# Edge passes of a graph-attention kernel: one accumulating transfer for two tiles, rings of six

## The reference

```python
def _gatv2(x, src, dst, Wl, bl, Wr, br, att, bias):
    xl = (x @ Wl + bl).reshape(N, H, C)
    xr = (x @ Wr + br).reshape(N, H, C)
    e = leaky_relu(xl[src] + xr[dst], 0.2)
    logits = einsum('ehc,hc->eh', e, att)
    m = segment_max(logits, dst)
    p = exp(logits - m[dst])
    s = segment_sum(p, dst)
    alpha = p / s[dst]
    return segment_sum(xl[src] * alpha[..., None], dst).reshape(N, H * C) + bias
```

## Time and profile before

| | us |
|---|---|
| median of 3 runs | 3033.68 |
| lowest and highest run | 3030.25, 3037.02 |
| profiled execution, its own time | 3031.11 |
| span of the profiled execution, first to last instruction | 3029.4 |
| busy: PE, DVE, ACT, POOL | 2627.9, 2517.6, 1696.8, 1318.7 |

### The profile page before, as it was taken

The page is one execution under the profiler, slowest core; times in us unless marked ns, Lnnn a source line. Parts: engine busy times, 40 slices in busy tenths (PEclk is TensorE's granted clock), DMA queues, the critical chain, the costliest instruction groups (busy, mean ns, idle before and its releaser), DMA issues. The chain is left out here.

```text
span 3029.4 us, 41062 instructions
## 1 busy us (share of the span) xinstructions
PE 2627.9 (87%) x11205; PEld 1800.7 (59%) x11205; DVE 2517.6 (83%) x5677; ACT 1696.8 (56%) x4291; POOL 1318.7 (44%) x1218
## 2 busy tenths in 40 slices
PE   6999999788888089999988888861899999969997
PEld 5777777333333078888864333320688888846665
DVE  7989998699999466677757999994988888469997
ACT  3545555277777433333323777774778877525554
POOL 0012220688887133333327888862333333014443
PEclk8999999899999599999999999985899999989998
DMA  8989999588887488888756888875999999469999
GB/s 321 341 305 320 319 324 339 185 233 240 236 240 209 116 274 276 268 269 264 263 200 205 235 240 239 241 188 169 386 357 354 348 345 346 148 176 252 249 252 158
DMA packets 332704, 789.73 MB, mean 261 GB/s; under 512 B 55118, under 2 KB 55664, under 8 KB 322266
## 3 DMA queue, kind: packets, MB, share of 16 engines
q1 hardware_dynamic: 220440, 540.20, 51.1%
q0 software_dynamic: 109584, 243.11, 33.4%
q10 hardware_dynamic: 2452, 3.79, 0.4%
HBM read 469.66 MB, written 329.28 MB: 264 GB/s over the span
## 5 line engine op out<-in xcount | busy, mean ns | idle before, releaser
L888 PE MATMUL bank<-wr,nT_e 128*128 128x512 f32 x1280 | 607.0, 619 | 0.5 <-DVE z_e L747 0.5
L1045 PE MATMUL bank<-whi,t_hi 128*128 128x512 f32 x1256 | 524.9, 418 | 23.9 <-DVE t_lo L406 23.9
L1047 PE MATMUL bank<-whi,t_lo 128*128 128x512 f32 x1256 | 499.3, 398 | 0.0
L1046 PE MATMUL bank<-wlo,t_hi 128*128 128x512 f32 x1256 | 498.9, 397 | 0.0
L888 PEld LDWEIGHTS bank<-wr,nT_e 128*128 128x128 f32 x1280 | 243.2, 200 | 250.5 <-issue 250.5
L912 POOL DMA_INDIRECT vin<-touched,node_slot x157 | 172.7, 1100 | 336.2 <-DMA vin<-rows 328.8
L912 POOL DMA_INDIRECT g_vin<-touched,node_slot x157 | 174.6, 1112 | 327.1 <-DMA g_xin<-in_x 303.7
L642 POOL DMA_INDIRECT nv_e<-rows,dst_row x160 | 209.9, 1312 | 175.5 <-POOLq L81 129.8
L1045 PEld LDWEIGHTS bank<-whi,t_hi 128*128 128x128 f32 x1256 | 237.9, 189 | 74.0 <-issue 17.4
L984 ACT CAST t_hi<-bank 128x512 fp32r<-128x512 f32 (+1 forms) x157 | 91.8, 585 | 329.7 <-PE bank L1047 329.6
L1047 PEld LDWEIGHTS bank<-whi,t_lo 128*128 128x128 f32 x1256 | 237.9, 189 | 58.8
(11 more groups left out here) (245 smaller groups left out, 6293.1 us busy)
## 6 DMA issues: line engine op xcount, KB each, us to landing
rows<-t_row SPq DMA_DIRECT2D x312, 512.0 KB, 4.4
w_e<-w_e POOLq DMA_DIRECT2D x160, 256.0 KB
touched<-done_e SPq DMA_DIRECT2D x160, 256.0 KB
xin<-in_x SPq DMA_DIRECT2D x156, 256.0 KB, 4.7
xTin<-in_xT SPq DMA_DIRECT2D x156, 256.0 KB
vin<-rows SPq DMA_DIRECT2D x156, 256.0 KB, 4.0
g_vin<-rows SPq DMA_DIRECT2D x156, 256.0 KB
g_xin<-in_x SPq DMA_DIRECT2D x156, 256.0 KB
```

The lines of the kernel that those rows point to most:

```text
L888: pe.matmul(psR[b][:, :], nT[:, b, cc, :], wr[:, cc, :], start=(cc == 0), stop=False)
L1045: pe.matmul(ps, hi[:, cc, :], whi[:, cc, :], start=(cc == 0), stop=False)
L1046: pe.matmul(ps, hi[:, cc, :], wlo[:, cc, :], start=False, stop=False)
L1047: last = pe.matmul(ps, lo[:, cc, :], whi[:, cc, :], start=False, stop=(cc == KC - 1))
```

## The change

The accumulating transfer is issued once for tiles 2u and 2u + 1, when the second of them is weighed (and for the last tile alone if their number is odd, which it isn't here). It covers two neighbouring slots of the rings, 4 KB in a partition. The rings have six slots, `w_added` has one semaphore for each pair of slots, and its starting value in layer 1 is counted for each pair. `accumulate` stands one turn later (lag G + 3 = 8).

```diff
-WR = 4
+WR = 6
...
-        g["w_added"] = [ctx.enter_context(nc.semaphore(f"w_added{u}")) for u in range(WR)]
+        g["w_added"] = [ctx.enter_context(nc.semaphore(f"w_added{u}")) for u in range(WR // 2)]
...
-        w_added, w0 = g["w_added"], layer * 16 * len(range(0, T, WR))
+        w_added, w0 = g["w_added"], [layer * 16 * len(range(2 * u, T, WR)) for u in range(WR // 2)]
...
             def add_own(t):
-                b = t % WR
+                if t % 2 == 0 and t < T - 1:
+                    return
+                b, n = t // 2 * 2 % WR, t % 2 + 1
                 pool.wait_ge(s["weighted"], t + 1)
-                pool.dma_start(w1[:, b, :], w2[:, b, :], accum_op=ALU.add).then_inc(w_added[b], 16)
+                pool.dma_start(w1[:, b:b + n, :], w2[:, b:b + n, :], accum_op=ALU.add).then_inc(w_added[b // 2], 16)
...
             def accumulate(t):
                 i, b = t // G, t % WR
-                dve.wait_ge(w_added[b], w0 + 16 * (t // WR + 1))
+                dve.wait_ge(w_added[b // 2], w0[b // 2] + 16 * (t // WR + 1))
...
-            lag = G + 2
+            lag = G + 3
```

## The result

The changed kernel takes 3017.46 us (median of five runs, 3016.2 to 3018.03), the kernel before 3033.01 beside it: a ratio of 0.9949, 95% interval 0.9936 to 0.9962. The profiled execution has a span of 3015.7 against 3029.4. The forecast was 3021, with 3000 to 3037 as its range. The time came out close, but not by the forecast's terms, as the rows show.

The account below looks back on a forecast made before the run. DVE was taken as the bound, with collisions behind POOL; -17.9 us from collisions and +5.8 at the ends make -12.1, from 3031.1 to 3019.0, and 2.6 for the median gives 3021 us, range 3000 to 3037.

Parts of the forecast that it names:

- What bounds, and the collision: DVE's loop: DVE is the bound; L757 stands behind POOL's L655, 1.12 us each, 32 times, 16 in a pass.
- The price of a double issue: L650 on POOL: issuing a transfer of two tiles costs 0.98 us, as a single one does; by tile 1.97.
- How many collisions go: DVE and POOL in the loops: 8 of 16 in a pass go, saving 17.9 us; bounds 12 to 20 in all.
- the start: Start of a pass: POOL still works off its lead of gathers, which may move the count by two or three either way.
- No wait for PE in the loop: DVE in the loop: it never waits for PE, whose 2.9 us to spare shrink to 0.9.
- PE starves: Rival, PE's gathers in the loop: DVE waits for PE once in ten tiles, 16 x 1 us: 3037; 0.17 with nothing gained.
- The later `accumulate` and the rings, at zero: DVE and ACT in the loop: moving `accumulate` a turn later and rings of six each change the time by zero.
- The ends of the passes: Serial end of each pass: costs 2.9 us a pass, 5.8 for both; bounds 2.4 to 10.
- the exponentials of the last group: ACT at the end of each pass: they come about 0.7 us later.
- the second `scale`: End of each pass: `scale(78)` must also wait for the last transfer, some +1.17 us.
- the transfer's growth: End of each pass: the last transfer carries two tiles, 256 KB more, +1.03 us.
- The sum: Whole kernel: -17.9 from collisions and +5.8 at the ends make -12.1 us.

Follow-up runs that it names:

- the long memset: The kernel before, with POOL's multiplication L655 replaced by a memset of a spare tile of 128 x 1344 elements: 3004.17 us, ratio 0.9905.
- the run on the ends: The changed kernel with a transfer of its own for each of the last two tiles of a pass: 3009.74 us, ratio 0.9923.

## Why the prediction was right

**What bounds, and the collision.** Right: an L655 with a lead, 1.12 us each. The long memset shows that a POOL which is merely busy and first does not do it.

**The price of a double issue.** Right: 0.96 us, where 0.98 was taken.

**How many collisions go.** The step that was mis-sized: 24 of 32 went, not 16, beyond the bounds of 12 to 20. Its reasoning holds in the steady part, where a collision is left once in ten tiles; with PE never late there are six a pass. What it missed lies at the start. The 16 of a pass are not one in each group of five: the first nine tiles have none, and four fall on tiles 9, 10, 13 and 14 (605.44 to 634.42 in pass 0). These eight of the 32 come where `accumulate` has hardly begun and a DVE turn can be as short as 4.07 us:

```profile
597.92 1.22 DVE L752 SCALAR_TENSOR_TENSOR z_e<-z_e 128x1024 f32<-128x1024 f32 x1
601.99 1.22 DVE L752 SCALAR_TENSOR_TENSOR z_e<-z_e 128x1024 f32<-128x1024 f32 x1
605.44 1.80 DVE L757 TENSOR_TENSOR z_e<-z_e,v_att 128x512 f32<-128x512 f32 x1
...
595.17 1.28 POOL L655 TENSOR_TENSOR z_e<-z_e,v_att 128x512 f32<-128x512 f32 x1 [0.96 <-DVE z_e L752]
600.20 1.31 POOL L655 TENSOR_TENSOR z_e<-z_e,v_att 128x512 f32<-128x512 f32 x1
605.39 1.30 POOL L655 TENSOR_TENSOR z_e<-z_e,v_att 128x512 f32<-128x512 f32 x1
```

A turn of POOL with a transfer is 5.03 to 5.19 us there, so that it falls behind by about one us a turn. In the changed kernel every second turn goes without, and takes 4.02 us (604.49 to 608.51): POOL never falls far enough back, and none of the eight is left. The forecast left half of them standing, and put the start down as two or three either way. That is four of the eight that went beyond the forecast; the other four are the places that became waits for PE.

**No wait for PE in the loop.** Wrong. The rival "PE starves" came about in part: 10.2 us in six waits, not 16 of 1 us. Its mechanism, that the gathers land later, is there, and by the forecast's 1.0 us (6.0 against 5.0 in the mean). By the forecast's sum that left PE 0.9 us of its lead. What no term held is PE's granted clock: with so little lead, the slow matmuls behind some of PE's waits (up to 2.6 us over 3.60) reach DVE. With the gathers a turn earlier the same slow matmuls cost nothing, so it takes both.

**The later `accumulate` and the rings, at zero.** Right of the rings in the loop as far as the times can tell (the loops of the two traces differ by 5.9 us, 830.7 with rings of four against 824.8), wrong of the `accumulate`: moving it costs 13 us by the medians, 16 between the profiled executions, against the same kernel with lag G + 2. It takes the longer turn away from where POOL needs it (9.3 - 1.7 = 7.6 us of collisions), PE's waits are 7.2 longer beside it, and the ends 4.4. DVE's own sum stays, as argued; what changes is who waits.

**The ends of the passes.** 4.6 us measured, 5.8 forecast, within the bounds. In pass 0 its parts are: the exponentials of the last group 0.97 later (7.78 us after the last `leaky` before, 8.75 after; 0.7 forecast), of which the later `accumulate` makes +1.90 and the larger ring -0.92; the second `scale` 1.17, as forecast; the transfer's growth 0.05 instead of 1.03, and its issue 0.45 sooner. That makes 1.74 of the 1.79 measured. In pass 1 the single of before took 3.86 us and the growth is 0.93. Against the faster single of the run on the ends (3.30) the pair is 1.5 to 1.6 us dearer, more than the forecast's 1.03, and far more than the 0.60 worked out beside it from the Trainium skill, "DMA: Bandwidth & Descriptors", section "Anatomy of one DMA". The forecast's error was to set its 1.03 on top of a single that took 4.84, and to take that for its usual time.

**The sum.** Right by offset, and that is luck: 9 us more from the collisions, 10 us lost to PE, 1 less at the ends.

## What to carry to other kernels

When two engines lock each other out, count the losses by looking for the instruction's long instances and the other's lead, and step through one period of the schedule with the durations of the rows, its beginning included; whether this change helped depended on which turn each piece of work fell into more than on how much work there was. Try each part of a change alone: here the part that carried the gain was worth 26 us by itself, and its two companions took 11 of them back. A transfer that is made larger can delay the ones queued beside it (here the gathers, from 5.0 to 6.0 us), so see whether those can go ahead in the same change.

## What the runs showed of the hardware

PE's granted clock fell around waits that are short beside the span: after standing for 2.58 us (before 683.80), 3.22 (847.99), 2.31 (1669.52) and 3.61 (1885.89) its four transposes took 1.11 or 1.12 instead of 0.66 us. After 2.64 us (before 815.20) the transposes still took 0.66, and the fall shows in the matmuls behind them:

```profile
815.20 0.66 PE L882 MATMUL bank<-ident,nv_e 128*128 128x128 f32 x4 [2.64 <-DMA vs_e<-rows,src_row]
815.69 5.30 PE L890 MATMUL bank<-wr,nT_e 128*128 128x512 f32 x8
```

Other waits of that length were followed by none of it (2.42 at 629.48 and 2.46 at 903.08: 0.66 and 3.60), so that the length alone does not tell. The kernel before had such falls too (2.15 us at 665.87, then 1.11 and 4.81), but DVE, held up by its collisions, hardly noticed (0.4 us in the loops). With the collisions taken away and nothing else of the transfers changed, in the long memset, DVE waits for PE by 6.7 us: a loss that was in part hidden by the one that the change removed.

An indirect issue is held while a DVE instruction with two inputs from SBUF runs (2.26 us instead of 0.98). The 41 L642 of the changed kernel that began during L748, which has one input in SBUF and one in a matmul's bank, took 0.96 to 0.98. A direct transfer's issue on the same engine is not held: L652 took at most 1.02 us in all 80 instances, and in the run with the transfer behind the gathers 33 of them began while L754 ran and took 1.00 to 1.05.
